# Experts and ternary network as single streams of products, and the loads of q and k pieces moved to the end of a step

## The reference

```python
# each of the 6 encoder layers; the rotary attention (L3_attn) has the same scores, softmax and values
scores = jnp.einsum('bhqd,bhkd->bhqk', q, k) * scale
scores = scores * smask
a = jax.nn.softmax(scores, axis=-1)
att = jnp.einsum('bhqk,bhkd->bhqd', a, v)
...
# mixture of experts: one shared network, and 8 experts weighed by the softmax of the two largest logits
shared = jnp.einsum('th,hd->td', jax.nn.silu(shared), shared_w2.T)
gate_logits = x_flat @ gate_w.T
h = jnp.einsum('td,ehd->teh', x_flat, experts_w1)
expert_out = jnp.einsum('teh,edh->ted', jax.nn.silu(h), experts_w2)
selected = jnp.einsum('ted,te->td', expert_out, gates)
...
# ternary network
h = jax.nn.silu(_tlin(x, w1_w, w1_s)) * _tlin(x, w2_w, w2_s)
h = jax.nn.gelu(_tlin(h, h1_w, h1_s), approximate=False)
h = jax.nn.gelu(_tlin(h, h2_w, h2_s), approximate=False)
return _tlin(h, w3_w, w3_s)
```

## Time and profile before

| | |
|---|---|
| Median of 3 runs | 5010.97 us (4997.11 to 5019.95) |
| Profiled execution, time | 5029.85 us |
| Its span | 5027.8 us |
| Mean granted clock of TensorE | 0.861 of full speed |
| Encoder | about 9 to 2257 us of the span |
| Experts | first product at 2272.65, `H` written at 2877.69 us |
| Ternary network | first product at 4228.49, `H` written at 4614.33 us |
| Rotary attention | from 4614.6, steps about 4673 to 4940 us |

### The profile page before, as it was taken

The page is one execution under the profiler, slowest core; times in us unless marked ns, Lnnn a source line. Parts: engine busy times, 40 slices in busy tenths (PEclk is TensorE's granted clock), DMA queues, the critical chain, the costliest instruction groups (busy, mean ns, idle before and its releaser), DMA issues. The chain is left out here.

```text
span 5027.8 us, 72866 instructions
## 1 busy us (share of the span) xinstructions
PE 3880.8 (77%) x27543; PEld 2644.1 (53%) x27543; DVE 2797.8 (56%) x6776; ACT 1896.4 (38%) x2957; POOL 786.3 (16%) x1074
## 2 busy tenths in 40 slices
PE   5898888888888888868898744477745566887986
PEld 3666666666666666656666511155423332333664
DVE  4756656746746647551212277788679773111663
ACT  2554554554545545533333233322212122221343
POOL 2212222222222122130000000000000031002221
PEclk8999999998999899988999866589857677998897
DMA  5414414423424324200000000000000000001431
GB/s 124 101 36 107 105 42 100 106 53 90 95 49 114 74 61 112 75 10 29 0 0 0 13 0 0 0 1 1 1 5 0 4 1 23 0 0 34 105 86 32
DMA packets 158830, 224.83 MB, mean 45 GB/s; under 512 B 17950, under 2 KB 138142, under 8 KB 141214
## 3 DMA queue, kind: packets, MB, share of 16 engines
q10 hardware_dynamic: 19656, 107.37, 9.7%
q1 hardware_dynamic: 138878, 113.45, 8.3%
HBM read 157.18 MB, written 63.57 MB: 44 GB/s over the span
## 5 line engine op out<-in xcount | busy, mean ns | idle before, releaser
L751 DVE TENSOR_REDUCE enc_mx<-psum 128x2 f32<-128x512 f32 (+1 forms) x1152 | 753.2, 686 | 408.4 <-PE psum L460 404.1
L892 ACT ACTIVATE enc_e<-psum 128x1024 f32<-128x1024 f32 (+1 forms) x768 | 580.7, 808 | 506.6 <-PE psum L479 446.5
L460 PE MATMUL psum<-enc_ks,enc_qs 80*128 80x128 bf16 (+1 forms) x3072 | 469.2, 259 | 126.0 <-DVE enc_mx L751 110.8
L479 PE MATMUL psum<-enc_qs,enc_ks 83*128 83x256 bf16 (+1 forms) x3072 | 393.2, 255 | 95.6 <-DMA enc_qs<-max_pieces 87.2
L460 PEld LDWEIGHTS psum<-enc_ks,enc_qs 80*128 80x128 bf16 x3072 | 224.6, 102 | 268.9 <-DVE enc_mx L751 174.6
L490 PE MATMUL psum<-enc_e,enc_v 128*32 128x256 f32 (+1 forms) x6144 | 347.7, 346 | 0.0
L479 PEld LDWEIGHTS psum<-enc_qs,enc_ks 83*128 83x128 bf16 x3072 | 263.1, 101 | 145.7 <-DMA enc_qs<-max_pieces 101.5
L1653 PEld LDWEIGHTS psum<-par_s,moe_act_h 128*128 128x128 f32 x2304 | 268.6, 192 | 26.8 <-issue 26.8
L1640 PE MATMUL psum<-cur,par_s 128*128 128x512 f32 x576 | 275.2, 625 | 0.0
L1717 ACT ACTIVATE moe_act_h<-psum 128x512 f32<-128x512 f32 x288 | 169.4, 598 | 273.5 <-PE psum L1640 272.9
L1653 PE MATMUL psum<-par_s,moe_act_h 128*128 128x128 f32 x2304 | 271.5, 275 | 0.0
(11 more groups left out here) (452 smaller groups left out, 7498.6 us busy)
## 6 DMA issues: line engine op xcount, KB each, us to landing
enc_qs<-q_pieces ACTq DMA_DIRECT2D x234, 192.0 KB
enc_ks<-k_pieces ACTq DMA_DIRECT2D x234, 192.0 KB
k_pieces<-enc_pieces SPq DMA_DIRECT2D x240, 128.0 KB, 2.0
q_pieces<-enc_pieces SPq DMA_DIRECT2D x144, 128.0 KB, 2.0
enc_qs<-q_pieces SPq DMA_DIRECT2D x54, 192.0 KB
enc_ks<-k_pieces SPq DMA_DIRECT2D x54, 192.0 KB
rope_qs<-q_pieces ACTq DMA_DIRECT2D x39, 192.0 KB
rope_ks<-k_pieces ACTq DMA_DIRECT2D x39, 192.0 KB
```

Of the source, the lines that this page charges most:

```text
L460: last = T_.matmul(p1[f % 2][:, i * kw:(i + 1) * kw], qs[0:KEYED, slot, h, j * P:(j + 1) * P], ks[0:KEYED, slot, h, 0:kw], start=True, sto ...
L479: last = T_.matmul(p2[ch][:, g], ks[0:SCORED, slot, 4 * T + g, ch * P:(ch + 1) * P], qs[0:SCORED, slot, 4 * T + g, 0:n], start=True, stop= ...
L751: V.tensor_reduce(mx[:, u % 2, j * HEADS + h0:j * HEADS + h0 + n], p1[f % 2].rearrange("p (h k) -> p h k", h=n), AX_X, ALU.max)\
L892: A.activation(e_of(T, ch), p2[ch], ACT.Exp, scale=HD ** -0.5).then_inc(s_e, 1)
```

## The change

1. Encoder and rotary attention: ACT issues `load` of sequence `u + 3` in part T = 3 of step `u`, behind the exponentials and behind `move_att` or `back`, and no longer in T = 0. The consumer, `fill(u + 3, 0)` in T = 0 of step `u + 1`, stays where it is.
2. Experts: the loops are gone. The 72 pairs of `up` and `down` (8 groups of 9 networks) run as one sequence on the PE, `up(n + 1)` ahead of `down(n)` across groups too. The PE reads `H` itself and no longer `cur`. The logits of group g + 1 stand behind `down` of e = 1 of group g, the transposes of group g - 1 behind e = 3; DVE does the statistics of g - 1 at e = 0, the scaling at e = 1, the ranking of g + 1 at e = 3, its weights at e = 6; ACT does the write-back and the exponential at e = 5. Sums, gates and normalisation buffers exist twice.
3. Ternary network: the same. The products up of group g + 1 stand in two halves between the hidden layers of group g and ahead of its products down; transposes and normalisation of g - 1 lie between the products of g.
4. Both stages now end with a barrier of all engines and the release of their semaphores, as the attention stages did already.

```diff
@@ encoder, ACT
-                        if T == 0 and u + 3 < SEQS:
-                            load(act, layer, 0, u + 3)
                         if T == 1 and u + 1 < SEQS:
                             fall(layer, 0, u + 1)
...
+                        if T == 3 and u + 3 < SEQS:
+                            load(act, layer, 0, u + 3)
@@ rotary attention, ACT
-                        if u + 3 < SEQS:
-                            load(act, u + 3)
...
+                    if T == 3 and u + 3 < SEQS:
+                        load(act, u + 3)
@@ experts, PE
+            choose(0)
+            up(0)
+            for n in range(RUNS):
+                g, e = n // E1, n % E1
+                if n + 1 < RUNS:
+                    up(n + 1)
+                down(n)
+                if e == 1 and g + 1 < GROUPS:
+                    choose(g + 1)
+                if e == 3 and g:
+                    turn(g - 1)
+            turn(GROUPS - 1)
@@ ternary network, PE
+            for g in range(GROUPS):
                 for f in range(FC):
+                    hidden(g, 0, f)
+                    if f == 0 and g:
+                        rows(g - 1)
+                for f in range(2):
+                    if g + 1 < GROUPS:
+                        up(g + 1, f)
+                for f in range(FC):
+                    hidden(g, 1, f)
+                    if f == 1 and g:
+                        turn(g - 1)
+                for f in range(2, FC):
+                    if g + 1 < GROUPS:
+                        up(g + 1, f)
+                pe.wait_ge(s_g, 2 * FC * (g + 1))
+                if g:
+                    pe.wait_ge(s_sum, g)
+                for k in range(FC):
+                    last = T_.matmul(bank[7], W["w3"][:, k * P:(k + 1) * P], h2[:, k], start=(k == 0), stop=(k == FC - 1))
```

More of the change, by code:

```diff
@@ L1620, in _ @@
         def _(pool):
-            with pool.Fori(0, GROUPS) as i:
-                fetch_group(c, pool, i + base, i)
-                norm_pool(c, pool, i + base)
+            for g in range(GROUPS):
+                N[g % 2].root(pool, g // 2)
         @block.tensor
         def _(pe):
-            W.wait(pe)
[L1628 to L1654, removed]
-                    last.then_inc(s_down, 1)
-                up(0)
-                for e in range(1, E1):
-                    up(e)
-                    down(e - 1)
-                down(E1 - 1)
-                norm_tensor(c, pe, i + base)
@@ new lines, in weigh @@
+            def weigh(g):
+                dve.wait_ge(s_exp, g + 1)
+                step(g, 7, V.scalar_tensor_tensor(out=weight[:], in0=rank[:], scalar=1.5, in1=weight[:], op0=ALU.is_lt, op1=ALU.mult))
+                step(g, 8, V.tensor_reduce(total[:], weight[:], AX_X, ALU.add))
+                step(g, 9, V.reciprocal(total[:], total[:]))
+                step(g, 10, V.tensor_tensor(gates[:, g % 2], weight[:], total[:].unsqueeze(2).broadcast_to(three), ALU.mult))
+            rank_experts(0)
@@ L1723 @@
+            back(GROUPS - 1)
+    return base
 BLK = 16
@@ L2345, in _, with rows, turn @@
+            def rows(g):
+                pe.wait_ge(s_sum, g + 1)
+                if g:
+                    pe.wait_ge(N[(g - 1) % 2].s_done, (g - 1) // 2 + 1)
+                for t in range(TILES):
+                    last = T_.transpose(bank[0][:, t * P:(t + 1) * P], y[:, g % 2, t * P:(t + 1) * P], c.ident)
+                last.then_inc(N[g % 2].s_rows, 1)
+            def turn(g):
+                N[g % 2].turn(pe, g // 2, bank[0])
             W.wait(pe)
-            with pe.Fori(0, GROUPS) as i:
-                pe.wait_ge(c.s_cur, i + (base + 1))
+            for f in range(FC):
+                up(0, f)
@@ L2391, in _, with back, move @@
+            def back(g):
+                act.wait_ge(N[g % 2].s_turned, g // 2 + 1)
+                A.activation(c.H[:, grp(g)], bank[0], ACT.Copy).then_inc(N[g % 2].s_done, 1)
+            def move(g):
+                if g >= 2:
+                    act.wait_ge(N[g % 2].s_normed, g // 2)
+                N[g % 2].move(act, g // 2, bank[0])
             W.wait(act)
-            with act.Fori(0, GROUPS) as i:
+            for f in range(FC):
+                gate(0, f)
+            for g in range(GROUPS):
@@ L2402, in _ @@
-                norm_scalar(c, act, i + base, ds(i * GROUP, GROUP))
-    return base + GROUPS
+                    gelu(g, 0, f)
+                    if f == 1 and g:
+                        move(g - 1)
+                for f in range(2):
+                    if g + 1 < GROUPS:
+                        gate(g + 1, f)
+                for f in range(FC):
+                    gelu(g, 1, f)
+                    if f == 3 and g:
+                        back(g - 1)
+                for f in range(2, FC):
+                    if g + 1 < GROUPS:
+                        gate(g + 1, f)
```

317 lines of the change are left out of this document (205 added, 112 removed).

## The result

The changed kernel takes 5707.24 us (median of 4 runs, 5702.96 to 5710.47) against 5004.85 us for the kernel before in the same session: a ratio of 1.140, 95% interval 1.137 to 1.143. The profiled execution took 5710.47 us, its span is 5708.7 us, the mean granted clock 0.811. The prediction was 5768 us, range 5520 to 5950.

What follows compares the result with a forecast made beforehand. The PE was taken as the bound, its order of products pacing the encoder's steps. -72 - 60 + 2 + 670 + 98 + 155 - 36 = +757 on 5029.85 us gave 5787, less 19 for the median: 5768 us, range 5520 to 5950.

Steps and rivals of the forecast that it cites:

- Streams: Experts and ternary network: the PE runs through without gaps between groups, gaining 72 and 60 us.
- the cover holds: Experts: DVE and ACT work for normalisation and logits fits beside the PE's products, so the PE need not wait.
- The stall, 670 us: Encoder: the PE stands each step until the load has landed, 111.7 us a layer, 670 us in six.
- the lead: Encoder: time from ACT's end of T = 3 to PE demand; 2.3 us after even steps, -0.35 odd, 4.2 at u = 1.
- The landing with stores, 11 us: Encoder, six even steps a layer: a load issued beside SP's stores lands in 11 us, between 9.5 and 12.3.
- the upper end: Encoder loads beside stores: engines serve queues in turn, landing in 12.3 us, the encoder's term growing by 47 us.
- The clock: Encoder and rotary attention: low PE clock behind each stall costs 1.7 us a step, 155 us over 91 steps.
- Rival 2: Attention steps: the clock stays at 0.50 for most of each step, 900 us more, 6650 us; chance 0.04.
- Relief in T = 0: Attention steps: issues taken out of ACT's T = 0 give back 0.4 us a step, 36 us in all.
- Rival 1: Attention steps: the stall is there but the rest of the step absorbs half of it, 5305 us; chance 0.07.
- The row of maxima: Encoder: the PE's DMA wait for it, 87.2 us before, stays or shrinks somewhat, since write and read-back meet no load.

Runs made afterwards that it cites:

- `streams_only`: Changed kernel with its loads of q and k pieces issued in T = 0 again, in both attentions; 4886.41 us, ratio 0.972 to the kernel before.
- `busy_stall2`: Changed kernel, with PE making 56 or 68 useless products while it stands before fill(u, 0) in the encoder, u >= 5; 5653.31 us, ratio 1.124.
- `loads_sp`: Changed kernel, with loads issued by SP once the exponentials of step u - 1 are through, none by ACT; 4847.03 us, ratio 0.9635.

## Why the prediction was right

The mechanism and the sign held, and the two stages of the streams to within 3 us. In the encoder the terms came out at other sizes, and their errors partly cancel: that the total is off by only 61 us is in part luck.

- **Streams** (-72, -60): measured -72.7 and -62.3. That the cover holds was the step that mattered, and the window without idle time shows it. `streams_only` puts the sum into the time.
- **The stall, 670 us: oversized.** Measured: 556 us of that wait, all of it new. The landing was taken as 8.8 us alone and 11 with stores; it was 9.4 (mean of 42 loads) and 10.0 (36). The larger error was the lead. The prediction had, as landing less growth, 0.5 us without stores (the mean of its five odd steps, one even step and u = 1) and 2.1 with them; measured, as landing less gap, 1.9 and 3.4. It let the issue begin when ACT had ended its last instruction of T = 3. The trace shows the issue at that instruction's start after odd steps (689.34, both rows, 0.78 us before its end), and after even ones 0.25 us ahead of that start, 0.86 before the end (713.03, with L900 at 713.28). So a step with stores lost 6.7 us, not 8.9 (36 of them), and one without 7.5, not 8.3 (42 in all). That is 80 + 34 = 114 us, the whole difference. The early issue explains 0.8 us a step of the lead's error of 1.3 to 1.4; the rest I can't assign.
- **The landing with stores, 11 us**, leaned to the sharing side. Sharing did cost, but 0.6 us and not 2.2. The Trainium skill's "DMA: Bandwidth & Descriptors", section "Queues, rings and completion order", lets an engine serve its queues in turn; by the upper end worked out beside it the stall would have been 47 us larger still, and the measured 10.0 lies well below it.
- **The clock** (133 us in the encoder): undersized. PE busy grew by 166.6 us there, 2.1 a step and not 1.7; in the turn shown the window behind the 4 us at 0.50 was not yet at full clock either (0.63). The prediction went by four steps that ran at 1.00 throughout; its show a turn that did not (1.06 us for four L479, against 0.6 at full clock). `busy_stall2` shows at least 1.1 us a step of it in the time. The mechanism is shown, its share of the length lies between these. Rival 2, a clock that never recovers, fell: the encoder's mean is 0.81.
- **Relief in T = 0** (-31 in the encoder): the PE's other waits as a whole fell by 23 us. Whether that is relief isn't shown: the weight loads that wait for the exponentials fell from 53.3 us to 38.5, but in `loads_sp`, where ACT issues nothing and there is no stall, they wait 53.5.
- **Rival 1**, half of it absorbed, fell: of a wait of 556 us the other waits gave back 23.
- **The row of maxima** was to wait as before or less: 86.5 us beside 87.2, as before. The write lands in 1.4 us where it took 2.7 (medians of 96), and from the read-back's issue to the PE it is 2.3 us where it was 2.2. Why the wait as a whole is no shorter stays open.

Against the sum: 772 predicted in the encoder, 699 measured. The stall was 114 too large, the clock 34 too small, and the other waits gave back 8 less than the relief. The total was 61 us too high, inside the range. From profile to profile it was 76 (757 predicted, 681 measured): the prediction took 19 us off for the distance of profile and median, and in the result the profiled run is only 3 above its median.

## What to carry to other kernels

Before a DMA is moved, put its landing beside the distance to its consumer, both from the trace; if the distance is below the landing, the difference is lost in every step, and what TensorE's low clock behind the stall costs comes on top. Count the distance from where the queue can issue, which here was up to 0.9 us ahead of the end of the instruction before it. Then look at what small transfer on a chain starts while it runs: the same load four us earlier was no longer late itself, but made the row of maxima late. A normalisation that is to hide in a stream of products has to stand clear of the point where it is just ready: 1.5 us too near cost 3 us a group, two networks further on cost nothing, and the place between was not run.

## What was not expected of the hardware

- A DMA of 24 KB issued while a load of 1152 KB is under way in another queue landed about when that load does: 9.7 and 9.9 us behind the load's start (to the next issue, medians of 78), issued 4.6 or 7.1 us behind it; alone it takes 1.4 us. Issued together with the load it took 3.3. The same section of the Trainium skill says that a semaphore's increment from a DMA engine lands only after every earlier write from that engine, across its queues. That fits; no run here tells it from plain sharing of the engines.
- A DMA issue on ACT's queue started while the ACTIVATE ahead of it still ran (both at 689.34), or before it (713.03 and 713.28).
- A wait of 1.45 us of the PE, behind 0.96 us of logits in a stream at clock 1.00, was followed by 4 us at 0.70 and 4 at 0.88; the same logits without the wait left it at 1.00.
